# Row sums of y's squares: four one-column products replaced by a transposing block sum on VectorE and one sixteen-column product

## The reference

```
r = sigmoid(x @ Wr.T); k = x @ Wk.T; v = x @ Wv.T          # x: (8, 2048, 256)
state = cumsum(k*v / scale, axis=time) * scale              # scale from sigmoid(decay)
y = r * state
y = y * rsqrt(mean(y*y, axis=-1) + 1e-6) * ln_w
x = layernorm(x + y @ Wo.T)
x = layernorm(x + gelu(x @ bw1.T + b1) @ bw2.T + b2)        # bw: signs of w times a mean |w| per row
```

## Time and profile before

| what | value |
|---|---|
| runs, lowest / median / highest | 835.35 / 835.58 / 835.84 us |
| span of the profiled execution, first to last instruction | 833.5 us |
| TensorE busy | 811.5 us (97%) |
| VectorE busy | 754.4 us (91%) |
| ScalarE busy | 679.1 us (81%) |
| GpSimd busy | 335.0 us (40%) |
| granted TensorE clock, mean | 0.999 |

### The profile page before, as it was taken

The page is one execution under the profiler, slowest core; times in us unless marked ns, Lnnn a source line. Parts: engine busy times, 40 slices in busy tenths (PEclk is TensorE's granted clock), DMA queues, the critical chain, the costliest instruction groups (busy, mean ns, idle before and its releaser), DMA issues.

```text
span 833.5 us, 16874 instructions
## 1 busy us (share of the span) xinstructions
PE 811.5 (97%) x5365; PEld 527.3 (63%) x5365; DVE 754.4 (91%) x1400; ACT 679.1 (81%) x971; POOL 335.0 (40%) x569
## 2 busy tenths in 40 slices
PE   6989999999999999999999999999999999999996
PEld 4555666666666666666666666666666666666663
DVE  6987999999999999999999999999999999999877
ACT  7886888888888888888888888888888888887775
POOL 3344333444333344333344333344433344433354
PEclk9999999999999999999999999999999999999999
DMA  8513553444553434554434554434454334444313
GB/s 247 104 30 77 128 114 90 99 103 101 126 126 81 103 93 101 126 126 90 107 80 107 120 126 101 100 80 108 113 126 107 94 87 109 106 101 101 77 26 101
DMA packets 169845, 86.27 MB, mean 103 GB/s; under 512 B 130144, under 2 KB 165472, under 8 KB 169824
## 3 DMA queue, kind: packets, MB, share of 16 engines
q1 hardware_dynamic: 148304, 52.97, 27.6%
q0 software_dynamic: 4608, 16.78, 10.4%
q10 hardware_dynamic: 16912, 16.26, 5.7%
HBM read 20.45 MB, written 16.78 MB: 45 GB/s over the span
## 4 chain that ended last, share of the span: by engine, by line
PE 90%; DVE 4%; ACT 2%; POOL 2%; DMA 1%; issue 1%; POOLq 0%; DVEq 0%; ACTq 0%; SPq 0%
PE ps_r L355 29%; PE ps_o L478 25%; PE ps_f L428 18%; PE ps_o L382 6%; PE ps_r L428 6%; PE ps_o L387 3%; PE ps_s L362 2%; DVE hid_lo L966 1%; DMA x_t<-x_st 1%; DMA x_in<-in_L_attn_x_dram 1%; ACT hid L657 0%; DVE u L917 0%; DVE u_st L925 0%; POOL root L1256 0%; ACT hid_hi L692 0%
## 5 line engine op out<-in xcount | busy, mean ns | idle before, releaser
L478 PE MATMUL ps_o<-w2T,hid_hi 128*128 128x256 f16 x992 | 218.9, 273 | 3.3 <-DVE hid_lo L966 2.9
L478 PE MATMUL ps_o<-w2T,hid_lo 128*128 128x256 f16 x992 | 218.8, 273 | 0.0
L355 PE MATMUL ps_r<-x_t,proj_hi 128*128 128x512 f16 x768 | 197.1, 379 | 1.4 <-DVE proj_lo L1042 1.2
L657 ACT ACTIVATE hid<-ps_f,b1c,f_scale 128x512 f32<-128x512 f32 x192 | 145.3, 774 | 54.7 <-PE ps_f L428 49.6
L428 PE MATMUL ps_f<-x_t,w1T 128*128 128x512 f16 x768 | 182.0, 379 | 2.3 <-DVE x_t L950 1.3
L1244 POOL TENSOR_TENSOR y_sqs<-y_sq 128x512 f32<-128x512 f32 x32 | 46.7, 1461 | 315.7 <-ACT y_sq L632 315.7
L966 DVE SCALAR_TENSOR_TENSOR hid_lo<-hid,hid_scale,hid_hi 128x1024 f16<-128x1024 f32 (+1 forms) x136 | 160.3, 1221 | 1.2 <-ACT hid_hi L692 0.6
L355 PEld LDWEIGHTS ps_r<-x_t,proj_hi 128*128 128x128 f16 x768 | 74.7, 98 | 91.3 <-issue 2.6
L692 ACT ACTIVATE hid_hi<-hid,hid_scale 128x2048 f16<-128x2048 f32 (+2 forms) x72 | 128.0, 1779 | 3.3
L428 PEld LDWEIGHTS ps_f<-x_t,w1T 128*128 128x128 f16 x768 | 75.0, 98 | 80.4 <-issue 2.6
L355 PE MATMUL ps_r<-x_t,proj_lo 128*128 128x512 f16 x384 | 114.2, 379 | 0.0
(11 more groups left out here) (176 smaller groups left out, 1380.4 us busy)
## 6 DMA issues: line engine op xcount, KB each, us to landing
x_in<-in_L_attn_x_dram SPq DMA_DIRECT2D x32, 512.0 KB, 3.9
res<-b_row POOLq DMA_DIRECT2D x32, 512.0 KB, 4.6
out_dram<-res ACTq DMA_DIRECT2D x31, 512.0 KB, 3.1
w_in<-in_L_ffn_w_dram SPq DMA_DIRECT2D x2, 1024.0 KB, 10.1
x_t<-x_st SPq DMA_TRANSPOSE x59, 4.3
b_row<-in_L_ffn_b_dram SPq DMA_DIRECT2D x1, 512.0 KB, 13.1
proj_in<-in_L_attn_Wk_dram SPq DMA_DIRECT2D x1, 256.0 KB, 5.2
proj_in<-in_L_attn_Wv_dram SPq DMA_DIRECT2D x1, 256.0 KB, 5.4
```

Source lines behind the costliest of these rows:

```text
L355: last = nc.tensor.matmul(ps_r[:, m, :], w[:, m, dc, ec * P:(ec + 1) * P], xx[:, :, dc, :], start=(n == 0), stop=(n == 3 * DC - 1))
L478: last = nc.tensor.matmul(o_tok[:, tt, :], hh[:, hc, tt * P:(tt + 1) * P], w2T[:, :, hc, :], start=(hc == 0 and n == 0), stop=(hc == HC - ...
L657: nc.scalar.activation(hid[:, hc, :], f1_bank[hc % NF], ACT.Gelu, bias=b1c[:, hc:hc + 1], scale=f1_scale[:, hc:hc + 1]).then_inc(s_gelu, 1)
```

## The change

VectorE gets a new instruction for each chunk, `block_sums`: a `tensor_reduce` of `y_sqs` with `apply_transpose`. It takes the 128x512 tile as blocks of 32x32 and sums, in each block, over the 32 partitions, with the block's 32 tokens laid on partitions. The result `y_part` is 128x16: for each quarter of the partitions its own partial sums of the sixteen groups of 32 tokens. TensorE then does one product with the constant 128x128 matrix `fold` as weights (four 32x32 identities in each direction) and `y_part` as the 16 moving columns. It adds the four quarters, and puts the result of each of the sixteen groups on all four quarters of the partitions. `mean_sq` takes of each row the one column out of four that belongs to its own quarter: it adds epsilon and multiplies with the mask `quarter` (which holds 1/256 or 0), waits for that, and sums the four columns. `fold`, `quarter` and `quarters` are made once, at the start, from the identity.

TensorE's product stands behind the third product of F1's tile 5, and waits for `y_part`; `block_sums` stands on VectorE between the second half of `zmul` and `zadd`.

```diff
+            def sum_rows(c):
+                pe.wait_ge(s_ypart, c + 1)
+                nc.tensor.matmul(ps_sums, fold[:, :, :].rearrange("p q t -> p (q t)"),
+                                 y_part[:, :, :].rearrange("p tt q -> p (tt q)"), start=True,
+                                 stop=True).then_inc(s_sums, 1)
 ...
-                            if sums_of is not None:
-                                sum_rows((2 * dc + n,))
+                            if sums_of is not None and dc == DC - 1 and n == 0:
+                                sum_rows(sums_of)
 ...
+            def block_sums(c):
+                dve.wait_ge(s_ysqs, c + 1)
+                nc.vector.tensor_reduce(y_part[:, :, :].rearrange("p tt q -> p (tt q)"),
+                                        y_sqs[:, :].rearrange("p (b t) -> p b t", t=P // TT), AX.X, ALU.add,
+                                        apply_transpose=True).then_inc(s_ypart, 1)
+
             def mean_sq(c):
                 dve.wait_ge(s_sums, c + 1)
-                nc.vector.tensor_scalar(ms[:, :], ps_s[:, 0:TT], 1.0 / D, 4.0 * EPS_RMS, ALU.mult,
-                                        ALU.add).then_inc(s_ms, 1)
+                nc.vector.scalar_tensor_tensor(out=ms_all[:, :, :], in0=ps_sums.rearrange("p (tt q) -> p tt q", q=TT),
+                                               scalar=4.0 * EPS_RMS * D, in1=quarter[:, :, :], op0=ALU.add,
+                                               op1=ALU.mult).then_inc(s_msall, 1)
+                dve.wait_ge(s_msall, c + 1)
+                nc.vector.tensor_reduce(ms[:, :], ms_all[:, :, :], AX.X, ALU.add).then_inc(s_ms, 1)
 ...
                 if left > 1:
                     zmul(i, (1,))
+                if left > 2:
+                    block_sums(i + 2)
+                if left > 1:
                     zadd(i, j)
 ...
+            pool.wait_ge(s_fold, 2)
+            nc.gpsimd.tensor_copy(fold[:, 1:TT, :], fold[:, 0:1, :].to_broadcast([P, TT - 1, P // TT]))
```

More of the change, by code:

```diff
@@ L63, in postln_layer_kernel @@
         ones_col = sb("ones_col", [P, 1])
+        quarters = sb("quarters", [P, TT])
         ones_sq = sb("ones_sq", [P, P])
@@ L77, in postln_layer_kernel @@
         diag = sb("diag", [P, DC, P])
+        fold = sb("fold", [P, TT, P // TT])
+        quarter = sb("quarter", [P, TT, TT])
+        y_part = sb("y_part", [P, TT, TT])
+        ms_all = sb("ms_all", [P, TT, TT])
         x_sq = sb("x_sq", [P, TT, D], bf16)
@@ L167, in postln_layer_kernel @@
         x_bank, x_split = [ps_r, ps_o, ps_f], [(x_hi, x_lo), (x1_hi, x1_lo), (x_hi, x_lo)]
-        ps_bounds = ps_s[:, TT:TT + DC + 1]
+        ps_sums = ps_s[:, 0:TT * TT]
+        ps_bounds = ps_s[:, TT * TT:TT * TT + DC + 1]
         bounds_16 = bounds[:, :].bitcast(bf16)[:, 1::2]
-        ps_wmax = ps_s[:, TT + DC + 1:TT + DC + 7]
+        ps_wmax = ps_s[:, TT * TT + DC + 1:TT * TT + DC + 7]
         ps_womax = ps_f[:, 0, 0:2]
@@ L200, in postln_layer_kernel @@
         s_sums, s_root = sem("sums_s"), sem("root_s")
+        s_fold, s_ypart, s_msall = sem("fold_s"), sem("ypart_s"), sem("msall_s")
         s_o, s_ms, s_rms, s_u = sem("o_s"), sem("ms_s"), sem("rms_s"), sem("u_s")
@@ L358, in R @@
                         last.then_inc(s_proj, 1)
[L360 to L365, removed]
+            def sum_rows(c):
[3 more added lines that the diff above has]
+                                 stop=True).then_inc(s_sums, 1)
             def O(c, k, last_chunk=False):
                 dst = o_last if last_chunk else o_tok
+                pe.wait_ge(s_yq, c + 1)
                 if k < 2:
-                    pe.wait_ge(s_ysqs, c + 1)
-                    pe.wait_ge(s_yq, c + 1)
-                    sum_rows(range(TT))
+                    sum_rows(c)
                 pe.wait_ge(s_yh, c + 1)
@@ L421, in F1 @@
                     if sums_of is not None:
-                        pe.wait_ge(s_ysqs, sums_of + 1)
                         pe.wait_ge(s_yq, sums_of + 1)
@@ L1045, in proj_split_lo @@
                                                op1=ALU.subtract).then_inc(s_setup_ev, 1)
+            dve.wait_ge(s_ident, 1)
+            nc.vector.tensor_reduce(quarters[:, :], ident[:, :].rearrange("p (q t) -> p q t", q=TT), AX.X,
+                                    ALU.add).then_inc(s_fold, 1)
+            dve.wait_ge(s_fold, 1)
+            nc.vector.tensor_scalar(quarter[:, :, :], quarters[:, :].rearrange("p (o q) -> p o q", o=1).to_broadcast(
+                [P, TT, TT]), 1.0 / D, None, ALU.mult)
+            nc.vector.tensor_reduce(fold[:, 0, :], ident[:, :].rearrange("p (q t) -> p t q", q=TT), AX.X,
+                                    ALU.add).then_inc(s_fold, 1)
             dve.wait_ge(s_decay_in, 16)
@@ L1129, in prologue @@
                 scans(1, 1, 0, y_second)
+                block_sums(0)
                 yl(0)
@@ L1144, in prologue @@
                 scans(2, 2, 0)
+                block_sums(1)
                 yl(1, y_second)
```

## The result

The changed kernel takes 822.44 us (median of 4 runs, 822.38 to 822.86), the kernel before 835.71 us in the runs beside it (835.35 to 835.84; the table further up gives 835.58, the second of the same four runs). The ratio is 0.9845, 95% interval 0.9831 to 0.9858: 13.3 us less. The profiled execution of the changed kernel is the slowest of the four, 822.86 us with a span of 821.0 us.

A forecast was written before the change was run, and what follows sets the result against it. TensorE's gap-free stream was taken as the bound. Span 833.5 - 11.9 (29 steps x 0.41) + 0.4 prologue + 0.2 last steps = 822.2 us; with 2.1 between span and median, 824.3 us, range 822.8 to 833.

The forecast's parts named there:

- What bounds the kernel: TensorE's gap-free stream sets the 24.86 us step; VectorE, busy 23.03 us, has 1.83 us to spare.
- TensorE in a step: Four small pairs cost 0.55 us, one new pair 0.14; 0.41 us a step removed, new step 24.45 us.
- The first rival: New product in tile 5 costs 0.25 us, so the step loses 0.30 instead of 0.41: 827.5 us, chance 0.08.
- block_sums: 0.60 forecast: VectorE's transposing reduce taken at a plain reduce's 0.60 us; upper bound the scan, 1.28; zadd 0.39 us later.
- The mean: VectorE's mean_sq becomes two instructions with a wait between: 0.28 us in place of 0.08, 0.20 more.
- VectorE's sum: VectorE gets 0.59 us more a step, with 0.86 us of waits to pay from; alone 24.2 us, under TensorE's 24.45.
- The tighter place: TensorE's first product with y_lo: y_lo is there 0.19 us early; from a block sum of 0.79 us TensorE waits.
- the second rival: Block sum of 0.8 to 1.1 us, or an unseen delay near y_lo, makes TensorE wait before `low`: 829.2 us, chance 0.12.
- The third, slower than before: Transposing reduce at half rate, 1.28 us: TensorE waits 0.49 us a step, more than it saves: 839.9 us, chance 0.12.
- the point of no gain: Block sum length from which the kernel gets slower: 1.2 us in the steps, 1.15 with the ends.
- The term `+0.4 us` of the sum: Prologue, chunk 1: y_lo 0.18 us late and the mean 0.20 more, on the chain through GpSimd's root.
- The last steps: Last chunk: the chain goes from the bounds to the root, so the mean's delay counts: +0.2 us.

The follow-up runs named there:

- extra_128: Changed kernel with one more transposing reduce of 128 columns per step into a tile nobody reads: 822.37 us, ratio 0.9844.
- old_prologue: Changed kernel, but chunks 0 and 1 get four products, no block sum and the one-instruction mean as before: 823.82 us, ratio 0.9861.
- dve_alone: Changed kernel with its new product made four times, at the places of the old four: 835.45 us, ratio 1.0001.
- the kernel padded with 36: Kernel before, with 36 idle products in TensorE's wait at its start: 836.59 us, ratio 1.0013.
- after_again: Changed kernel run once more, no edit: 822.39 us, ratio 0.9844.

## What of the forecast held, and the step that failed

**What bounds the kernel: right.** TensorE's stream set the step before and sets it after. Taking away TensorE's three pairs without adding VectorE's work gives the same step (24.445), adding VectorE's work without taking the pairs away gives the old one (24.856).

**TensorE in a step: right to 0.01 us.** Forecast 24.45, measured 24.446. The new pair was taken at 0.14 and takes 0.14. The first rival, a costlier product, did not appear.

**block_sums: 0.60 forecast, 0.63 measured**, with zadd 389.59 - 388.35 = 1.24 us behind zmul (forecast 1.21). The row of the plain reduce was the right neighbour, and the scan far off. The estimate of 1.24 us from the Trainium skill ("VectorE: DVE Perf Modes", "The three transpose paths") isn't borne out here: a block transpose inside a reduce costs 0.03 us over the plain reduce. The page's figure itself, 311 ns for 128x128, is near what the smallest addition shows (301 ns for 128 columns, `extra_128`). What failed is taking it four times: 256 columns take 430 ns and 512 take 701, about 1.04 ns for each further column on some 170 ns that don't grow. That page's tier table, by which tensor_reduce goes at the plain rate, agrees: 256 columns more (0.63 against 0.36) cost 0.27 us, 1.05 ns each, and 128 columns 0.23.

**The mean: right in the large.** The second instruction starts 0.20 us after the first, as reckoned.

**VectorE's sum: the working was wrong on the safe side.** The forecast gave VectorE 0.59 us of work more a step and found 0.86 to pay from, so about 0.3 us of waits should be left. Measured are 0.47 for y_q and some 0.04 for the rest. Waits fell from 1.27 to 0.51, by 0.76, of which 0.41 is TensorE's earlier arrival: the change cost VectorE only 0.35. Two things go into this. One is seen: `y_lo` is not later at all behind y_q, where 0.03 was reckoned, since block_sums fills its idle time. The other is worked out: an instruction that needn't wait starts about 0.08 us before the one ahead of it has ended (block_sums 0.61 behind a zmul of 0.69, 388.35 to 388.96; the prediction took this 0.61 from the earlier trace rows, whose lines don't show it), one that waits doesn't. Each wait that goes gives this back; three went (k_sb, y_lo, x_st), which is 0.24 us, the difference between 0.59 and 0.35. No run isolates it. `zadd` is also 0.04 us shorter on average (1183 ns against 1225).

**The tighter place: right.** `y_lo` was forecast to have 0.19 us to spare, and has 0.22. The three kernels with an extra block sum find this threshold from outside: nothing at 0.12, 0.02 at 0.26, 0.29 at 0.52. So the second rival is a true mechanism, only not at this block sum's length. The third, slower than before, would have needed more than it was given. At twice the block sum's cost the kernel still takes 831.26 us, 4 less than before, so a VectorE held for 0.63 + 0.59 = 1.22 us isn't the point of no gain that the working put at 1.15 to 1.2. There TensorE was to wait 1.22 - 0.79 = 0.43 us a step and loses 0.29: 0.03 because the time to spare was 0.22 and not 0.19, 0.03 because the single block sum holds VectorE for 0.63 and not 0.60, and 0.07 because `y_lo` still had that much idle time left behind zadd (1.17 from start to start in the changed kernel, 1.10 here).

**The prologue: this step failed.** The term `+0.4 us` of the sum was wrong in sign. It put the mean's delay on the chain in full, and let TensorE's wait for x1's transfer stand. By it the second F2 of the loop starts at 87.34 + 0.4 - 0.41 = 87.33. It starts at 85.93, 1.40 earlier, so the prologue gives back 1.0 us instead of costing 0.4. Two parts:

- *The mean's delay was hidden.* The root is later by 0.21 us (51.12 against 50.91), or 0.33 of the 0.4 reckoned, since the chain ahead of it is 0.12 us earlier. (Not through O of chunk 0: `old_prologue` and `dve_alone`, with four products there, are as early, and the changed kernel's one product waits 0.6 us for y_part.) But the residual that the delay should have pushed does not follow: it starts at 52.69, where it started at 52.82. VectorE's timeline, before and then after:

```profile
51.44 1.28 DVE L966 SCALAR_TENSOR_TENSOR hid_lo<-hid,hid_scale,hid_hi 128x1024 f16<-128x1024 f32 x1 [0.61 <-ACT hid_hi L692]
52.82 0.48 DVE L917 SCALAR_TENSOR_TENSOR u<-ps_o,rms,x_in 128x256 f32<-128x256 f32 x1
```
```profile
51.31 1.28 DVE L981 SCALAR_TENSOR_TENSOR hid_lo<-hid,hid_scale,hid_hi 128x1024 f16<-128x1024 f32 x1 [0.28 <-ACT hid_hi L697]
52.69 0.48 DVE L932 SCALAR_TENSOR_TENSOR u<-ps_o,rms,x_in 128x256 f32<-128x256 f32 x1
```

Hid_lo of chunk 0 ends at 52.72 and at 52.59, and both times the residual starts 0.10 us behind it. That holds in all thirteen profiles on record (0.09 to 0.10 us), though the root starts anywhere between 50.49 and 51.67. GpSimd's rms, which runs beside hid_lo, ends 0.05 to 0.07 us behind it each time: it took 0.78 us before, takes 0.45 now, and 0.29 in `dve_alone`, where the root is latest against hid_lo. So the later root only shortened rms, which ends with hid_lo either way. The working followed the chain of waits and did not ask what stood on VectorE at the moment the root was ready.

- *A wait that the forecast left standing went.* TensorE's 0.71 us for x1's transfer, and 0.16 because a product that doesn't wait starts before the modelled end of the one ahead (the chain's 68.47 against 68.31), are 0.87; with the 0.13 they make the 1.00 by which F1 starts sooner, and with the forecast's 0.4, the 1.40. The transfer went from 6.0 us to 4.3. It was never asked why it took 6.0; before, it stood on the last chain with 5.99 us. Taking the prologue back brings the long transfer back (+1.4 us in all, 1.10 of it in front of the second F2), and so do 12 idle products (+1.2, of which 0.77).

What is shown is that 24 instructions at the start of TensorE's program are enough to turn this transfer from 4.3 into 6.0 us, and that the time of its issue isn't what decides. That the cause is the instruction packet in front of the transfer's last descriptors is an inference from its times. In all six kernels with the long transfer (6.0 to 6.2 us) the packet comes 3.79 to 3.93 us after the issue; in the seven with the short one (3.7 to 4.3) none comes then. The nearest is the changed kernel's own, at 3.64 us; the others' come behind the transfer's last packet. In all six long ones the packet takes 0.89 or 0.94 us, and the transfer's two late packets start when it ends, to 0.02 us. That supports the inference, and so does the second long transfer of the kernel padded with 36. But the changed kernel's packet takes 1.18 us and nothing of the transfer comes late behind it, so a packet near the transfer's end isn't enough by itself. And the last packet is only 1.0 us later after the issue (4.8 against 3.8), the landing 1.7.

Open are, beside these 0.7 us, two things: why the packet keeps so closely to 3.8 or 3.9 us after the issue, even in the padded kernel before, where both came 0.7 us later (it may itself be waiting behind the transfer's packets), and whose instructions it carries. The Trainium skill ("Runtime: NRT & Kernel Launch", "Instruction fetch mechanics") says that an engine's sequencer fetches its instructions in blocks of 16 KiB over a DMA queue of its own, and that this is mostly hidden. The packet's 0.02 MB agree with that size; that it is hidden doesn't hold here, if the inference does.

**The last steps: +0.2 forecast, and the mean's 0.2 is there.** From y_q to the start of the last norm the way is 0.20 us longer (37.60 before, 37.80 after, 37.78 in `after_again`). What follows is no part of the change: from the start of the last norm to the end of the span it is 833.5 - 829.69 = 3.8 us before and 821.0 - 816.99 = 4.0 after, but 820.5 - 816.86 = 3.6 in `after_again`, the same kernel.

**Adding up.** The span was forecast at 822.2 and is 821.0: -1.40 in the prologue, +0.2 behind the last norm. (In `after_again`, 820.5: -1.52 and -0.2.) Around the span lie 1.86 us instead of 2.1, which gives 822.86 for the profiled execution; the 2.1 set the median of the runs against the span of another, faster one. The other three runs are 0.3 to 0.4 shorter in span. The mechanism and the size of the main term were right, and the range was too narrow below: 822.8 allowed nothing for a wait in the prologue that could go. The forecast had two priced ways up for the prologue and none down.

## What to carry to other kernels

Where one engine's stream is gap-free, taking a small f32 product from it is worth what its two passes hold (0.137 us here, whatever the columns), and the engine that takes the work over must be checked at the one place where the first waits for it, not by its total slack: 0.22 us there decided, with 1 us free in the step. A transfer that takes 6 us on the chain of before is a term of its own: ask what sets it, and give the range room for its going. And ahead of a delay on the chain, look at what the receiving engine is doing at that moment.

## What the hardware showed that was not expected

- A tensor reduce that transposes in 32x32 blocks sums over partitions at the rate of a plain one: 0.70 us for 128x512 in f32, 0.63 from start to start, 0.59 when it follows another.
- GpSimd's small steps stretch beside two of VectorE's instructions, and end just behind them. Before, y_inv ran beside `zadd` (395.63, zadd from 395.51), took 1.16 us and ended 0.05 behind it. Now it runs beside the block sum (389.29, before zadd's 389.59) and takes 0.19. U_neg runs beside hid_lo and ends 0.05 us behind it in both kernels; it went from 0.68 to 0.31 us on average. Over the kernel GpSimd is busy 39 us less, with one instruction more. Both zadd and hid_lo read two tiles in SBUF; that this is what holds GpSimd up was not tested.
- A transfer of the same bytes took 4.3 us without and 6.0 us with 24 more instructions at the start of another engine's program (one profile with them, two without; all four runs with them are slower than all eight without).
- At the start, the instruction that makes `fold` from the identity (128x128) took 1.44 us and the one for `quarter` (128x16) 1.52, while the one before them, over the same 128x128, took 0.29. Why wasn't looked into; it stayed hidden, as VectorE's next instruction started at 3.33 us as before.
